# Other paces for the attention and layer-norm units woven into the wo and wb matmuls of an eight-core sandwich layer

## The chip, the cores and the metric

The kernel runs on the 8 cores of one Trainium2 chip. Each core handles 2048 of the 16384 tokens, with all the weights, and no core waits for another. The time is the device time of the slowest core in microseconds.

## The reference

```python
x = hidden_states                      # (4, 4096, 4096), fp32
h = layernorm(x)
q, k, v = h @ Wq.T, h @ Wk.T, h @ Wv.T # each (.., 64 heads, 64)
q, k, v = q * mask_q, k * mask_kv, v * mask_kv
scores = einsum('bshd,bsgd->bshg', q, k) / 8     # heads against heads, token by token
out = einsum('bshg,bsgd->bshd', softmax(scores), v)
x = x + layernorm(out @ Wo.T)
h = layernorm(x)
base = h @ W_base.T + b_base
# top-2 of 8 experts by h @ W_router.T, rank-16 LoRA per expert
lora = einsum('ter,te,eor->to', einsum('td,erd->ter', h, A), w, B) * 2
x = x + layernorm(base + lora)
```

The attention is between the 64 heads of one token, so each token stands alone. It is many small products: 64 x 64 scores per token.

## The kernel before

Each core works through its 2048 tokens in 2 chunks of 1024 (`for c in range(NCH)`), and each chunk in 8 tiles of 128 tokens (tau 0 to 7). LNT holds the chunk's normalised activations, transposed, in bf16. A weight matrix is read in 64 pieces: 8 column blocks of 512 (n) times 8 groups of 512 rows (ktg). A piece goes into one of four buffers WG. In chunk 0 a piece comes by a casting DMA from the fp32 weights on POOL and is saved as bf16 by SP (`s_wo<-WG`); in chunk 1, and in the second half of a chunk, it is read back by SP (`WG<-s_wo`). A group, below, is the set of matmuls with one piece: 32 matmuls of 128x512 in the QKV stage (L341), 16 in the wo stages (L590) and wb stages (L763), which take four tiles at a time and so four of the eight PSUM banks.

The stages of a chunk, in order:

- layer norm and transposes of all tiles, then the 192 QKV groups.
- attention of tiles 0 to 3 alone (`drain(a3_units(range(0, 4), 16, ...))`).
- first wo stage: 64 groups for tiles 0 to 3 (`proj_half`), and woven into it the attention of tiles 4 to 7 from the generator `gen_h1`, with what is left of it drained afterwards.
- second wo stage: 64 groups for tiles 4 to 7, and woven into it `a5_b0_units` for tiles 0 to 3 (two layer norms, transposes, router).
- first wb stage: six units of `moe_tail_units` (tile 4) ahead, then 64 groups for tiles 0 to 3; the rest of `moe_tail_units` (tiles 5 to 7 and the LoRA products) is woven into the first 8 groups, n = 0, and whatever is left is drained at the end of n = 0.
- second wb stage: 64 groups for tiles 4 to 7, with the final layer norm of tiles 0 to 3 (b6) beside them.

The weaving is by generators. Each `yield` ends a unit, and `drive(gen, k)` appends k units to the instruction lists after a group. There is no scheduler behind it: every engine runs its list in order and waits on semaphores, so the place of a unit in the lists decides which matmuls stand between two steps that depend on each other.

The attention of a tile has 54 units: two batches of 32 token pairs (bt = 0 and 1) of 26 units each, then the read of the result (`BFN<-on`, on POOL) and the transposes into LNT. A batch begins with one unit of eight DMAs on SP (QSG, KB and VB, L148) and ends with one unit that stores OB. Between them stand four waves of six units. The text calls the matmuls of a wave Q (L407), K (L427), S (L446), P (L487) and O (L506); the sixth unit has only VectorE's work on OB (L520). Q is copied to QBD by VectorE (L416), K to KTS by ScalarE (L435), S needs both; P waits for the maximum (L464) and the exponentials (L470); O waits for a copy by ScalarE (L494); the next Q waits for L520 of the wave before. Four tiles make 216 units.

A tile of `a5_b0_units` has six units: the reads of T2 and XT with the first layer norm; the residual sum, the store of xp and the second layer norm; the transposes (L278); the router logits (L645); the gating on VectorE (L651 to L672); the matmul and copy to WTS (L677, L680). The first read of T2 waits for every APST store of the wo stage before it.

After the eighth group of a column block ScalarE copies four banks to APST (L601), and POOL stores them; the units driven after that group come before these copies in the lists.

Of the kernel before, what the change touches and what calls it, by code (L numbers as in the profile page):

```python
# [26 lines left out]
def _build_program():  # L27
# [25 lines left out]
    ap_d = nc.dram_tensor("apn", [CH, DM], F32, kind="Internal").ap()  # L53
# [243 lines left out]
    for c in range(NCH):  # L297
      try:
# [257 lines left out]
        def drive(gen, k):  # L556
            for _ in range(k):
                if next(gen, "END") == "END":
                    return False
            return True  # L560

        def drain(gen):
            for _ in gen:
                pass
# [3 lines left out]
        a35h0_v, a35h0_s = cnt["V"], cnt["S"]  # L568
# [1 line left out]
        ph(4, c)  # L570
        ap_i = [0]

        def proj_half(nm, taus, banks, src, gen, img_d, first_waits=()):
            for n in range(NB):
                for ktg in range(8):
                    b, rdy = load_wgroup(nm, n, ktg, src)
# [16 lines left out]
                                 waits, inc="T" if (k4 == 3 and ti == len(taus) - 1) else None)  # L593
                    wg_done(b, "T", cnt["T"])
                    if gen is not None:
                        drive(gen, 3)
                tmm = cnt["T"]
                for ti, tau in enumerate(taus):
                    sl = ap_i[0] % 4
# [8 lines left out]

        gen_h1 = a3_units(range(4, 8), 8, (4, 5, 6, 7))
        proj_half("wo", [0, 1, 2, 3], [0, 1, 2, 3], src_kind0, gen_h1, ap_d,  # L610
                  [("V", a35h0_v), ("S", a35h0_s)])
        drain(gen_h1)
        g_set("LNTa", ("T", cnt["T"]))
        a4h0_ap = [(f"ap{i}", cnt[f"ap{i}"]) for i in range(4)]
        a4h0_vs = [("V", cnt["V"]), ("S", cnt["S"])]
# [69 lines left out]

        gen_a5h0 = a5_b0_units(range(0, 4), (0, 1, 2, 3))
        a4h1_ap = [None]
        proj_half("wo", [4, 5, 6, 7], [4, 5, 6, 7], "scratch", gen_a5h0, ap_d, a4h0_vs)
        a4h1_ap[0] = [(f"ap{i}", cnt[f"ap{i}"]) for i in range(4)]
        drain(gen_a5h0)  # L690
        g_set("LNTb", ("T", cnt["T"]))
# [51 lines left out]
        def b1_half(taus, banks, src, gen):  # L743
            for n in range(NB):
# [5 lines left out]
                for ktg in range(8):  # L750
# [16 lines left out]
                                 inc="T" if (k4 == 3 and ti == len(taus) - 1) else None)  # L767
                    wg_done(b, "T", cnt["T"])
                    if gen is not None:
                        drive(gen, 3)  # L770
                if gen is not None:
                    drain(gen)
                for ti, tau in enumerate(taus):
# [21 lines left out]
        gen_moe = moe_tail_units()  # L795
        drive(gen_moe, 6)
        b1_half([0, 1, 2, 3], [0, 1, 2, 3], src_kind0, gen_moe)
        drain(gen_moe)
        b1h0_y = [(f"ap{i}", cnt[f"ap{i}"]) for i in range(4)]
# [15 lines left out]

        b6_units(range(0, 4), b1h0_y)
        b1_half([4, 5, 6, 7], [4, 5, 6, 7], "scratch", None)
        g_set("LNTa", ("T", cnt["T"]))
        g_set("LNTb", ("T", cnt["T"]))
# [60 lines left out]
```

How the kernel before makes its waits and increments, by code:

```python
        def run(eng):  # L826
            for waits, fn, inc, amt in sched[name]:
                for s_, v_ in waits:
                    eng.wait_ge(sems[s_], v_)
                instr = fn(eng)
                if inc is not None:
                    instr.then_inc(sems[inc], amt)
```

## Time and profile before

| | us |
|---|---|
| median of 2 runs | 8694.74 |
| the runs | 8647.36, 8742.12 |
| profiled execution | 8209.84 |
| its span on the slowest core (core 7) | 8208.3 |
| spans of the eight cores | 8147.3 to 8208.3 |
| TensorE busy, share of the span | 5385.0, 66% |
| VectorE, ScalarE, POOL busy | 1492.6, 774.4, 496.2 |

The profile is one execution, taken apart instruction by instruction on the slowest core. The span runs from the first to the last instruction; the execution's own time is 1.5 us longer. The granted clock is the share of 2.4 GHz that TensorE was given: 1.00 is 2.4 GHz, 0.50 is 1.2 GHz, and a value between is a mean over time at both levels. An idle time in brackets stands before the first instruction of a row, with what ended it. The ends of matmuls are modelled, so that a matmul seems to overlap the next by a little.

### The profile page before, as it was taken

What the parts mean: (1) busy time and instruction counts of PE and PEld (TensorE: products, weight loads), DVE (VectorE), ACT (ScalarE), POOL (GpSimd) and SP (SyncE); (2) the same over time, 40 slices, a digit from 0 to 9 for tenths busy, and PEclk for the clock granted to TensorE, in tenths of its full rate; (3) what the DMA queues carried; (4) which work ended last, traced back from release to release, by engine and by line L of the source; (5) the groups of instructions that cost most, each with busy time, mean ns of one, the idle gap of its engine ahead of it and who ended that gap; (6) DMA issues with size and microseconds to landing.
All of it is one profiled execution on the core that took longest, in us unless ns stands there. A gap on an engine that the chain in (4) does not pass through costs nothing.

```text
span 8208.3 us, 69959 instructions; the slowest of 8 cores (8147.3 to 8208.3 us)
## 1 busy us (share of the span) xinstructions
PE 5385.0 (66%) x28056; PEld 2554.0 (31%) x28056; DVE 1492.6 (18%) x2144; ACT 774.4 (9%) x1427; POOL 496.2 (6%) x785
## 2 busy tenths in 40 slices
PE   4888888842345457564918888888822565476964
PEld 2333333322222223221403333333322232233321
DVE  4000000023212251302051000000033222504012
ACT  1000000012112210000010000000022122100000
POOL 1000000000001000111000000000000000000110
PEclk7999999965677778787958999999955787697987
DMA  6666666632566655797552222222222433555655
GB/s 149 141 146 144 141 144 141 141 76 52 96 137 133 133 192 185 174 197 233 173 205 71 77 77 77 77 77 77 77 49 52 113 102 94 196 183 163 213 184 191
DMA packets 940079, 1084.79 MB, mean 132 GB/s; under 512 B 575217, under 2 KB 792306, under 8 KB 923378
## 3 DMA queue, kind: packets, MB, share of 16 engines
q0 software_dynamic: 225872, 492.98, 26.3%
q1 hardware_dynamic: 713890, 587.34, 23.7%
q8 instruction: 229, 3.75, 0.2%
q14 instruction: 88, 0.72, 0.0%
HBM read 885.23 MB, written 369.10 MB: 153 GB/s over the span
## 4 chain that ended last, share of the span: by engine, by line
PE 58%; DMA 15%; DVE 11%; SPq 6%; ACT 6%; issue 3%; POOL 1%; DVEq 0%; ACTq 0%; POOLq 0%
PE PALL L341 33%; PE PALL L590 11%; PE PALL L763 8%; SPq L148 6%; DVE BN L192 4%; DMA WG<-wbT 2%; DMA T<-yn 2%; ACT QBD L494 2%; ACT PSTG L470 2%; DMA VB<-vn 2%; DMA T<-apn 1%; DMA WG<-woT 1%; PE PALL L278 1%; PE PALL L487 1%; PE PALL L407 1%
## 5 line engine op out<-in xcount | busy, mean ns | idle before, releaser
L341 PE MATMUL PALL<-WG,LNT 128*128 128x512 bf16 x12288 | 2787.8, 389 | 404.3 <-DVE QST L359 108.1
L341 PEld LDWEIGHTS PALL<-WG,LNT 128*128 128x128 bf16 x12288 | 1222.6, 100 | 1969.0 <-issue 601.5
L590 PE MATMUL PALL<-WG,LNT 128*128 128x512 bf16 x4096 | 1034.8, 413 | 190.0 <-DMA WG<-woT 92.2
L763 PE MATMUL PALL<-WG,LNT 128*128 128x512 bf16 x4096 | 937.7, 390 | 122.3 <-DMA WG<-wbT 113.6
L278 PE MATMUL PALL<-idt,BFN 128*128 128x128 bf16 x1536 | 168.9, 308 | 837.3 <-DVE BFN L204 608.8
L590 PEld LDWEIGHTS PALL<-WG,LNT 128*128 128x128 bf16 x4096 | 419.1, 105 | 747.9 <-issue 370.3
L763 PEld LDWEIGHTS PALL<-WG,LNT 128*128 128x128 bf16 x4096 | 404.5, 100 | 642.7 <-issue 203.3
L192 DVE BATCH_NORM_STATS2 BN<-T 128x6 f32<-128x512 f32 x320 | 193.5, 675 | 1695.4 <-DMA T<-yn 1244.9
L359 DVE TENSOR_TENSOR QST<-PALL,maskK 128x512 bf16<-128x512 f32 x128 | 80.7, 685 | 2053.6 <-PE PALL L341 2011.2
L278 PEld LDWEIGHTS PALL<-idt,BFN 128*128 128x128 bf16 x1536 | 158.6, 145 | 852.1 <-issue 852.1
L435 ACT ACTIVATE KTS<-PALL 128x512 bf16<-128x512 f32 x192 | 104.2, 594 | 3077.3 <-PE PALL L427 3077.3
L407 PE MATMUL PALL<-idt,QSG 128*128 128x128 bf16 x1024 | 103.7, 272 | 358.0 <-DMA VB<-vn 351.1
L416 DVE CAST QBD<-PALL 128x512 bf16<-128x512 f32 x256 | 162.0, 685 | 777.4 <-PE PALL L407 777.4
L487 PE MATMUL PALL<-idt,PSTG 128*128 128x128 bf16 x1024 | 102.6, 270 | 241.8 <-ACT PSTG L470 241.8
L359 DVE TENSOR_TENSOR QST<-PALL,maskV 128x512 bf16<-128x512 f32 x128 | 80.8, 685 | 987.9 <-PE PALL L341 950.3
L407 PEld LDWEIGHTS PALL<-idt,QSG 128*128 128x128 bf16 x1024 | 88.8, 125 | 378.6 <-issue 367.7
L470 ACT ACTIVATE PSTG<-PALL,NM 64x512 bf16<-64x512 f32 x256 | 167.8, 679 | 294.2 <-DVE NM L464 171.0
L481 DVE TENSOR_REDUCE ZW<-PSTG 128x8 f32<-128x1024 bf16 (+1 forms) x96 | 151.2, 1575 | 199.9 <-ACT PSTG L470 199.9
L290 DVE CAST LNT<-PALL 128x512 bf16<-128x512 f32 x192 | 132.9, 692 | 292.1 <-PE PALL L278 291.7
L785 ACT ACTIVATE APST<-PALL 128x512 f32<-128x512 f32 x128 | 76.2, 597 | 1037.6 <-PE PALL L780 1033.6
L148 POOL DMA_DIRECT2D BFN<-on x16 | 8.6, 536 | 2735.3 <-DMA on<-OB 2735.3
L776 PE MATMUL PALL<-bbn,onesb 1*128 1x512 bf16 x128 | 50.9, 398 | 181.6 <-DMA bbn<-bb 181.6
(99 smaller groups left out, 2149.3 us busy)
## 6 DMA issues: line engine op xcount, KB each, us to landing
WG<-s_wo SPq DMA_DIRECT2D x192, 512.0 KB, 3.6
WG<-s_wb SPq DMA_DIRECT2D x192, 512.0 KB, 3.8
XT<-x POOLq DMA_DIRECT2D x24, 2048.0 KB, 9.7
WG<-wqT POOLq DMA_DIRECT2D x64, 512.0 KB, 5.7
s_wq<-WG SPq DMA_DIRECT2D x64, 512.0 KB, 3.3
WG<-wkT POOLq DMA_DIRECT2D x64, 512.0 KB, 5.7
s_wk<-WG SPq DMA_DIRECT2D x64, 512.0 KB, 3.0
WG<-wvT POOLq DMA_DIRECT2D x64, 512.0 KB, 5.8
```

The lines of the kernel that those rows point to most:

```text
L148: return emit(eng, lambda e, o=out, i=in_: e.dma_start(out=o, in_=i), waits, inc=sem, amt=16)
L192: emit("vector", lambda e, i=i: e.bn_stats(BN[:, 6 * i:6 * i + 6], src_ap[:, 512 * i:512 * i + 512]), (list(vwaits) + g_w("MV") + g_w("BN" ...
L278: emit("tensor", lambda e, bk=bk, kt=kt, off=off: e.matmul(pb(bk, off * 128, 128), src_sb[:, kt * 128:kt * 128 + 128], idt[:], start=True, ...
L341: e.matmul(pb(tau, 0, 512), LNT[:, colk(kt, tau):colk(kt, tau) + 128], WG[b][:, k4 * 512:k4 * 512 + 512], start=st, stop=sp),
L359: ev = emit("vector", lambda e, tau=tau, sl=sl, mk=mk: e.tensor_tensor(QST[:, sl * 512:sl * 512 + 512].rearrange("p (h d) -> p h d", d=64) ...
L407: emit("tensor", lambda e, j=j, jj=jj, p=p, qb_bk=qb_bk: e.matmul(pb(qb_bk[j // 4], (j % 4) * 128, 128), QSG[p][:, jj * 128:jj * 128 + 128 ...
L416: emit("vector", lambda e, pw=pw, bk=bk, i_=i_: e.tensor_copy(QBD[pw][:, i_ * 512:i_ * 512 + 512], pb(bk, 0, 512)), [("T", t_s0)] if i_ == ...
L470: s_s6 = emit("scalar", lambda e, a=a, pw=pw, bk_i=bk_i, sb_=s_bk[bk_i]: e.activation(PSTG[pw][64 * a:64 * a + 64, bk_i * 1024:bk_i * 1024 ...
L487: emit("tensor", lambda e, j=j, pw=pw, ptb=pt_bk[j // 4], po=(j % 4) * 128: e.matmul(pb(ptb, po, 128), PSTG[pw][:, j * 128:j * 128 + 128], ...
L494: emit("scalar", lambda e, pw=pw, bk=bk, i_=i_: e.activation(QBD[pw][:, i_ * 512:i_ * 512 + 512], pb(bk, 0, 512), AF.Copy), [("T", t_s7)] ...
L590: e.matmul(pb(bk, 0, 512), LNT[:, colk(kt, tau):colk(kt, tau) + 128], WG[b][:, k4 * 512:k4 * 512 + 512], start=st, stop=sp),
L763: e.matmul(pb(bk, 0, 512), LNT[:, colk(kt, tau):colk(kt, tau) + 128], WG[b][:, k4 * 512:k4 * 512 + 512], start=st, stop=False), waits,
```

## The change

`proj_half` takes a number of units per group as an argument. The first wo stage drives 6 attention units after each group instead of 3, the second wo stage 1 layer-norm unit instead of 3, and the first wb stage 1 instead of 3. No instruction is added or removed; only the order of the lists changes.

```diff
-        def proj_half(nm, taus, banks, src, gen, img_d, first_waits=()):
+        def proj_half(nm, taus, banks, src, gen, img_d, first_waits=(), pace=3):
...
                     if gen is not None:
-                        drive(gen, 3)
+                        drive(gen, pace)
...
         proj_half("wo", [0, 1, 2, 3], [0, 1, 2, 3], src_kind0, gen_h1, ap_d,
-                  [("V", a35h0_v), ("S", a35h0_s)])
+                  [("V", a35h0_v), ("S", a35h0_s)], pace=6)
...
-        proj_half("wo", [4, 5, 6, 7], [4, 5, 6, 7], "scratch", gen_a5h0, ap_d, a4h0_vs)
+        proj_half("wo", [4, 5, 6, 7], [4, 5, 6, 7], "scratch", gen_a5h0, ap_d, a4h0_vs,
+                  pace=1)
...
                     if gen is not None:
-                        drive(gen, 3)
+                        drive(gen, 1)
```

TensorE, first wo stage of chunk 0, from the transposes of tile 3 on (one row of L590 x16 is one group; the names of the other rows are those given above), before:

```order
L278 MATMUL PALL<-idt,BFN 128x128 x32
L590 MATMUL PALL<-WG,LNT 128x512 x16
L407 MATMUL PALL<-idt,QSG 128x128 x8
L427 MATMUL PALL<-idt,KB 128x64 x8
L590 MATMUL PALL<-WG,LNT 128x512 x16
L446 MATMUL PALL<-KTS,QBD 128x64 x8
L487 MATMUL PALL<-idt,PSTG 128x128 x8
L506 MATMUL PALL<-VB,QBD 128x64 x8
L590 MATMUL PALL<-WG,LNT 128x512 x16
L407 MATMUL PALL<-idt,QSG 128x128 x8
```

The same place in the changed kernel:

```order
L278 MATMUL PALL<-idt,BFN 128x128 x32
L590 MATMUL PALL<-WG,LNT 128x512 x16
L407 MATMUL PALL<-idt,QSG 128x128 x8
L427 MATMUL PALL<-idt,KB 128x64 x8
L446 MATMUL PALL<-KTS,QBD 128x64 x8
L487 MATMUL PALL<-idt,PSTG 128x128 x8
L506 MATMUL PALL<-VB,QBD 128x64 x8
L590 MATMUL PALL<-WG,LNT 128x512 x16
L407 MATMUL PALL<-idt,QSG 128x128 x8
```

The group between K and S is gone; the one between O and the next Q stays.

TensorE, from the last transposes of the attention in the first wo stage of chunk 0 into the second wo stage, before:

```order
L506 MATMUL PALL<-VB,QBD 128x64 x8
L278 MATMUL PALL<-idt,BFN 128x128 x32
L590 MATMUL PALL<-WG,LNT 128x512 x16
L278 MATMUL PALL<-idt,BFN 128x128 x32
L590 MATMUL PALL<-WG,LNT 128x512 x16
L645 MATMUL PALL<-wrT_s,LNT 128x8 x32
L677 MATMUL PALL<-idt,WBF 8x128
L590 MATMUL PALL<-WG,LNT 128x512 x16
L278 MATMUL PALL<-idt,BFN 128x128 x32
```

and in the changed kernel:

```order
L506 MATMUL PALL<-VB,QBD 128x64 x8
L278 MATMUL PALL<-idt,BFN 128x128 x32
L590 MATMUL PALL<-WG,LNT 128x512 x496
L278 MATMUL PALL<-idt,BFN 128x128 x32
L590 MATMUL PALL<-WG,LNT 128x512 x16
L645 MATMUL PALL<-wrT_s,LNT 128x8 x32
L590 MATMUL PALL<-WG,LNT 128x512 x32
L677 MATMUL PALL<-idt,WBF 8x128
L590 MATMUL PALL<-WG,LNT 128x512 x48
L278 MATMUL PALL<-idt,BFN 128x128 x32
```

The 496 matmuls are 31 groups: 28 of the first wo stage, behind the end of the attention, and three of the second. In the second stage two groups now stand before L677 and three before the next tile's transposes, where one stood.

TensorE, first wb stage of chunk 0, from its first group to the LoRA products (L700 and L724, in the changed kernel L701 and L725), before:

```order
L763 MATMUL PALL<-WG,LNT 128x512 x16
L278 MATMUL PALL<-idt,BFN 128x128 x32
L763 MATMUL PALL<-WG,LNT 128x512 x16
L645 MATMUL PALL<-wrT_s,LNT 128x8 x32
L677 MATMUL PALL<-idt,WBF 8x128
...
L763 MATMUL PALL<-WG,LNT 128x512 x16
L700 MATMUL PALL<-WTS,rep 128x512 x2
L724 MATMUL PALL<-LNT,WG 128x512 x64
L763 MATMUL PALL<-WG,LNT 128x512 x16
```

and in the changed kernel:

```order
L764 MATMUL PALL<-WG,LNT 128x512 x48
L278 MATMUL PALL<-idt,BFN 128x128 x32
L764 MATMUL PALL<-WG,LNT 128x512 x16
L645 MATMUL PALL<-wrT_s,LNT 128x8 x32
L764 MATMUL PALL<-WG,LNT 128x512 x32
L677 MATMUL PALL<-idt,WBF 8x128
L764 MATMUL PALL<-WG,LNT 128x512 x32
L278 MATMUL PALL<-idt,BFN 128x128 x32
...
L677 MATMUL PALL<-idt,WBF 8x128
L701 MATMUL PALL<-WTS,rep 128x512 x2
L725 MATMUL PALL<-LNT,WG 128x512 x64
```

All eight groups of n = 0 now stand before the transposes of tile 6.

## Rows read from the trace of the kernel before

**Rows 1.** View of the cores: span and mean granted clock of the slowest.

```profile
core 7: 8208.3 us, clock 0.814
```

**Rows 2.** Windows of core 7: stretch, its length, busy time by engine, clock, DMA.

```profile
core 7: us, PE busy (x) PEld busy (x) DVE busy (x) ACT busy (x) POOL busy (x), PEclk, DMA share, GB/s
2139.00:2811.60 672.60, 344.25 (x2240) 172.04 (x2238) 122.98 (x180) 120.49 (x208) 61.72 (x91) 0.76 0.68 137
2811.60:2880.30 68.70, 17.36 (x193) 13.93 (x194) 19.15 (x28) 18.50 (x32) 3.78 (x7) 0.53 0.43 122
6384.60:6941.50 556.90, 341.35 (x2243) 168.46 (x2244) 122.99 (x180) 120.50 (x208) 16.58 (x31) 0.82 0.41 106
6941.50:7001.20 59.70, 16.80 (x193) 13.40 (x189) 19.15 (x28) 18.55 (x32) 3.73 (x7) 0.55 0.36 125
2880.30:3228.30 348.00, 253.03 (x1284) 118.78 (x1284) 100.00 (x160) 29.36 (x64) 20.25 (x38) 0.87 0.52 178
3275.00:3433.00 158.00, 68.41 (x398) 34.14 (x397) 78.05 (x125) 13.56 (x31) 17.66 (x26) 0.72 0.65 176
7395.70:7536.70 141.00, 69.77 (x398) 34.69 (x398) 77.80 (x125) 12.55 (x30) 6.30 (x10) 0.71 0.44 144
7173.40:7348.20 174.80, 168.53 (x766) 74.38 (x765) 0.00 (x0) 10.38 (x21) 11.91 (x23) 1.00 0.55 178
```

**Rows 3.** Timeline of TensorE, drained attention of chunk 1: start, length, instructions, idle before.

```profile
6961.68 1.01 PE L407 MATMUL PALL<-idt,QSG 128*128 128x128 bf16 x8 [1.22 <-DVE OB L520]
...
6964.35 0.58 PE L446 MATMUL PALL<-KTS,QBD 128*128 128x64 bf16 x8 [1.33 <-ACT KTS L435]
6967.35 1.01 PE L487 MATMUL PALL<-idt,PSTG 128*128 128x128 bf16 x8 [2.41 <-ACT PSTG L470]
...
6971.39 1.01 PE L407 MATMUL PALL<-idt,QSG 128*128 128x128 bf16 x8 [1.12 <-DVE OB L520]
```

**Rows 4.** Timeline of TensorE, first wo stage of chunk 1, batch with bt = 0.

```profile
6404.38 5.58 PE L590 MATMUL PALL<-WG,LNT 128*128 128x512 bf16 x16
...
6410.56 3.63 PE L590 MATMUL PALL<-WG,LNT 128*128 128x512 bf16 x16
...
6419.16 5.02 PE L590 MATMUL PALL<-WG,LNT 128*128 128x512 bf16 x16
```

**Rows 5.** Timeline of TensorE, same stage, batch with bt = 1.

```profile
6481.20 3.62 PE L590 MATMUL PALL<-WG,LNT 128*128 128x512 bf16 x16
...
6492.87 3.62 PE L590 MATMUL PALL<-WG,LNT 128*128 128x512 bf16 x16
```

**Rows 6.** Timeline, same stage, between the batches with bt = 0 and bt = 1.

```profile
6465.44 2.93 SPq L148 DMA_DIRECT2D VB<-vn  x2
...
6473.97 4.91 PE L590 MATMUL PALL<-WG,LNT 128*128 128x512 bf16 x16 [19.73 <-DMA WG<-s_wo]
```

**Rows 7.** Timeline, end of the last attention tile of chunk 1.

```profile
6980.92 1.70 SPq L148 DMA_DIRECT2D on<-OB  x2
...
6996.85 3.57 PE L278 MATMUL PALL<-idt,BFN 128*128 128x128 bf16 x32 [16.87 <-DMA BFN<-on]
```

**Rows 8.** Timeline of TensorE, chunk 0: first wo stage, then two column blocks of wb.

```profile
2420.43 5.86 PE L590 MATMUL PALL<-WG,LNT 128*128 128x512 bf16 x16 [14.47 <-DMA WG<-woT]
...
3532.12 9.83 PE L763 MATMUL PALL<-WG,LNT 128*128 128x512 bf16 x32 [11.72 <-DMA WG<-wbT]
...
3562.92 3.61 PE L763 MATMUL PALL<-WG,LNT 128*128 128x512 bf16 x16 [0.92 <-DMA WG<-wbT]
...
3581.05 9.27 PE L763 MATMUL PALL<-WG,LNT 128*128 128x512 bf16 x32 [11.96 <-DMA WG<-wbT]
```

**Rows 9.** Timeline, second wo stage of chunk 0 and what follows it.

```profile
2931.61 0.53 POOL L148 DMA_DIRECT2D T<-apn  x1
...
2939.66 3.57 PE L278 MATMUL PALL<-idt,BFN 128*128 128x128 bf16 x32 [17.71 <-DVE BFN L204]
...
2974.43 3.57 PE L278 MATMUL PALL<-idt,BFN 128*128 128x128 bf16 x32 [18.03 <-DVE BFN L204]
...
3265.87 3.57 PE L278 MATMUL PALL<-idt,BFN 128*128 128x128 bf16 x32 [37.52 <-DVE BFN L204]
```

## The prediction

> **What bounds the kernel now.** I read the view of the cores first: core 7 ends last, at 8208.3 us, with a mean granted clock of 0.814 [rows 1]; the profiled execution took 8209.84 us. All eight cores run the same program and lie within 61 us of each other, so one core can be read for all. Next I read the stages in windows [rows 2]. The change touches three stages of each chunk. In the wo stage of the first half (64 groups of 16 matmuls, with the attention of the other half woven in) the kernel spends 672.60 us and then 68.70 us in what is left of the attention (chunk 0), and 556.90 and 59.70 us (chunk 1). In the wo stage of the second half it spends 348.00 us, and in the first eight wb groups 158 us (chunk 0) and 141 us (chunk 1). The reader should set this against the dense stretch in rows 2: 174.80 us for 48 groups, 3.64 us a group, at a granted clock of 1.00. At that price 64 groups are 233 us, so the first wo stage is not a matmul stage. It is a chain: attention steps that wait for one another, with groups between them.
>
> How that chain is covered shows in the timeline. With no group in it a wave of eight heads takes 9.71 us from Q to Q, and TensorE waits 1.33 us for KTS and 2.41 us for the exponentials on its way [rows 3]. In the batches with bt = 0 the pace of 3 puts one group between O and the next Q, and one between K and S: 14.78 us a wave, in which the first group takes 5.58 us (it starts at the 1.2 GHz level after the light work) and the second 3.63 us (2.4 GHz level) [rows 4]. In the batches with bt = 1 the groups stand at S/P and at O/Q, and a wave with two groups takes only 11.67 us [rows 5]. So two groups there cost 2 us more than none: they are almost free.
>
> **The change: pace 6 in the first wo stage.** 216 units at 6 a group are gone after 36 groups instead of 64 groups and a drain of 24 units. So 28 groups lose their attention neighbours. I count what the attention part gets shorter by, and add the 28 groups.
>
> Batches with bt = 0, 16 waves in all four tiles: the group between K and S goes (3.6 us), but the wait for KTS and QBD that it hid comes back (1.4 us, after 1.33 in rows 3). 14.8 − 3.6 + 1.4 = 12.6 us, so 2.2 us less, 35 us in all.
>
> Batches with bt = 1: one group stays, between S and P. 9.71 − 2.41 (hidden) − 0.5 (P runs at the higher level) + 5.5 (a group that starts at the lower level, rows 4) = 12.3 us. Twelve waves stood at 11.67: +7 us. The four of the last tile ran without a group at 9.71: +10 us.
>
> Between bt = 0 and bt = 1 SP must first issue the store of OB and eight reads of 128-byte pieces. In chunk 1 the next group's weights are queued behind them on SP, so TensorE is idle 19.73 us and then runs that group before Q [rows 6]. After the change Q, K, S come first and need only the reads: the wait stays, the group (about 5 us) leaves it: −20 us over four tiles. In chunk 0 the weights come through POOL, the group lies in the shadow of the reads, and I count 0. At the end of a tile nothing changes: from the store of OB to the transposes pass 16 us of stores and reads [rows 7], in which TensorE has no part, so a group beside them neither shortens nor lengthens them.
>
> The 28 groups afterwards: in chunk 1 28 × 3.64 = 102 us. In chunk 0 each group needs a 1 MB cast load from POOL. The wb stage of chunk 0 shows what such groups cost with nothing woven in: from 3532.12 to the end of the eighth group, 3566.5, is 34.4 us, 4.3 each, and then TensorE waits 11.96 us at the column boundary, because the next loads stand on POOL behind four stores that wait for ScalarE [rows 8]. 28 × 4.3 = 120 us. The three boundaries among them are not new; before, the same boundary cost 14.47 us amid the attention [rows 8], so −6 us.
>
> Chunk 1: −35 + 7 + 10 − 20 + 102 = +64 us. Chunk 0: −35 + 7 + 10 − 6 + 120 = +96 us. Together +160 us.
>
> **Pace 1 in the second wo stage.** VectorE runs two layer norms a tile; from one tile's transposes to the next 34.77 us pass, and TensorE waits 18.03 us of them for BFN [rows 9]. Now one group stands between transposes and logits, two before WTS, three before the next transposes. The layer norms of the next tile are queued on VectorE behind the WTS copy, so the two new groups before WTS (7.5 us) delay them, less the 3.5 us of gating that they hide, plus 1 us for groups that start cold: 39.8 us a tile, but with 6 groups in it instead of 2. The first transposes come later: nothing is drained ahead, so T2 can only be read once the last APST stores have landed. The same chain from the end of the second wo stage takes 3265.87 − 3228.3 = 37.6 us [rows 9]. Fourth transposes at 37.6 + 3 × 39.8 = 157.0; then 3.6 for the transposes, 43 groups × 3.64 = 156.5 and 2.4 for logits, WTS and the cold start: 319.5 us against 348.0. −28.5 us a chunk, −57 us.
>
> A page of the Trainium skill speaks against me here: "SBUF — State Buffer", section "SBUF: two separate sides", says that a DMA issued from GpSimd cannot get its descriptors written while VectorE runs an operation of a two-port mode, and would put these loads behind the layer norms. In the trace the POOL DMAs beside the layer norms take 0.53 us, as everywhere [rows 9], and none waits for VectorE except where the program says so. By the page, up to 2.4 us would be lost at each of some eight cast loads of the wb stage in chunk 0, 20 us; by the row, nothing, and I take the row.
>
> **Pace 1 in the first eight wb groups.** The unit sequence must be drained at the end of n = 0 as before. Of the eight groups three now stand before the first transposes, one before the logits, two before WTS and two before the second transposes; the last two tiles run without any. Where VectorE's layer norms are waited for, groups cost nothing, before as after; what remains is that the last two groups of the eight (some 6 and 3.6 us by rows 4), which stood behind the last WTS and uncovered, are gone from there, against about 1 us more ahead of it: −9 us a chunk, −18 us. In chunk 0 POOL holds cast loads behind xp stores that wait for VectorE, before as after.
>
> **Sum.** 160 − 57 − 18 = +85 us on 8209.84. The median of the runs shown, 8694.74, is 1.059 of that execution; I scale the difference too: +90 us, 8785 us (+1.0%).
>
> **Rivals.**
> 1. *The groups stay at the higher level, not slower.* The one group a wave takes 5.5 us in my sum, and 3.6 us if the clock does not fall in the light work ahead of it. 72 groups × 1.9 = 137 us less: −52, scaled −55, 8640 us. It decides the sign: below 4.3 us a group the change does not lose. For it: the paced stretches of rows 5 keep 3.62 us. Against it: rows 4, where 5 us of light work were enough for a slow group, and rows 2, where the stretches of attention alone have 0.53 and 0.55.
> 2. *The groups run almost wholly at the lower level.* At 6.4 us each (twice 3.62 would be 7.2), 72 × 0.9 = +65: +150, scaled +159, 8854 us. For it: the light work between groups grows from 5 to over 7 us. Against: the group after the long wait in rows 6 takes 4.91. The Trainium skill's page "TensorE: Matmul & The Clock Gate", section "HAM oscillation — how this bites in real kernels", has this mechanism: bursts of sixteen matmuls parted by waits each start throttled again. By it every one of the 72 groups starts cold; my sum already has that, and the rival is only its full length.
> 3. *Pace 1 covers nothing in the second wo stage:* the layer norms slip by as much as the groups fill. Then 57 us are missing: +142, scaled +150, 8845 us. Against it stands the 18.03 us wait in rows 9, longer than three groups.
>
> **How the numbers follow.** Forecast 0.55, rival 1 0.17, rival 2 0.18, rival 3 0.10. The forecast's own range is 8725 to 8850: the 5.5 us may be 4.8 to 6.0, the reads of rows 6 vary by some us a batch, and the cast groups may cost 4.0 to 4.8 us. The whole range takes in rivals 1 and 2 with some room: 8630 to 8895. 2% of 8694.74 is 174 us, about what a measurement of this kernel tells from no change. Over it lie two thirds of rival 2 and a little of rival 3 and of the forecast: 0.17. Under −174 us only a case better than rival 1: 0.06. Within: 0.77.
>
> **What would show each step.** First wo stage of chunk 1 up to the end of its last group: 680 us by my sum (556.90 + 59.70 + 64), with the 28 dense groups at 3.64 us and 12 to 13 us from group to group before. Chunk 0: about 837 us in place of 741. Second wo stage: 320 us, with 40 us from transposes to transposes. Wb: the eighth group followed by n = 1 at 132 (chunk 1) and 149 us (chunk 0). I am wrong if the woven groups show 3.6 us, if the dense ones of chunk 0 run at the pace of chunk 1, or if the first wo stage gets shorter.

## The result and the profile after

The changed kernel takes 8501.22 us (median of 12 runs, 8297.42 to 8880.37), the kernel before, measured again beside it, 8531.78 us (median of 10 runs, 8217.97 to 8817.83). The ratio is 1.0096, with a 95% interval of 1.0077 to 1.0114: about 1% slower, which is no difference at the 2% bound; the two medians themselves differ by 31 us the other way. In many executions of either kernel the cores of one or both dies ran at a lower granted clock for a part of the time; the ratio leaves these out (among them the two runs shown before the prediction, 5% and 6% above the lowest), and where a stage below is given for some cores only, or a time is called the lowest, this is why.

In the profiled execution the cores of the changed kernel need 8252.6 to 8308.3 us, the ones of before 8147.3 to 8208.3 us. The view of the cores for the changed kernel (span and mean granted clock), against [rows 1]:

```profile
core 1: 8308.3 us, clock 0.806
...
die 0 (median of its cores): 8273.0 us, clock 0.809
die 1 (median of its cores): 8282.7 us, clock 0.808
```

The median over the eight cores is 8274.3 us against 8191.6 us: +83 us. The page of each kernel has the projections' matmuls in one group of its table of costly groups (instructions, busy us and mean ns of one, then idle time ahead of them). Before, then after:

```profile
L590 PE MATMUL PALL<-WG,LNT 128*128 128x512 bf16 x4096 | 1034.8, 413 | 190.0 <-DMA WG<-woT 92.2
```
```profile
L590 PE MATMUL PALL<-WG,LNT 128*128 128x512 bf16 x4096 | 1076.3, 426 | 161.1 <-DMA WG<-woT 103.1
```

The same 4096 matmuls are busy 41 us longer, and TensorE waits 29 us less ahead of them. This group mixes both wo stages, so it has to be taken apart by stage. Windows of core 1 of the changed kernel: chunk 0, first wo stage with attention woven in, then its dense tail; the same for chunk 1; the second wo stages of both chunks; the first eight wb groups with what is queued beside them, of both chunks. They answer to [rows 2].

```profile
core 1: us, PE busy (x) PEld busy (x) DVE busy (x) ACT busy (x) POOL busy (x), PEclk, DMA share, GB/s
2141.10:2813.00 671.90, 288.12 (x1984) 149.39 (x1984) 142.14 (x208) 130.74 (x224) 37.79 (x56) 0.67 0.48 94
2813.00:2978.20 165.20, 110.70 (x448) 45.35 (x448) 0.00 (x0) 8.26 (x16) 26.39 (x40) 0.83 0.93 199
6462.10:6993.80 531.70, 287.70 (x1984) 147.08 (x1985) 141.45 (x207) 129.96 (x223) 10.70 (x20) 0.71 0.34 84
6993.80:7098.70 104.90, 98.84 (x453) 43.50 (x451) 0.69 (x1) 9.04 (x18) 7.49 (x15) 1.00 0.52 169
2978.20:3306.00 327.80, 247.33 (x1284) 115.69 (x1284) 99.92 (x160) 29.00 (x64) 22.96 (x41) 0.88 0.58 202
7098.70:7422.50 323.80, 248.34 (x1284) 115.80 (x1284) 99.91 (x160) 29.00 (x64) 23.71 (x42) 0.88 0.61 207
3352.80:3518.20 165.40, 74.42 (x398) 33.91 (x398) 77.78 (x125) 13.45 (x31) 16.84 (x25) 0.65 0.64 166
7471.90:7607.90 136.00, 65.53 (x399) 33.62 (x398) 77.79 (x125) 13.31 (x31) 7.07 (x11) 0.70 0.47 145
```

The 448 matmuls of the second row are the 28 groups that lost their neighbours, the 453 of the fourth row the same in chunk 1. In chunk 1 they cost 104.90 us at a granted clock of 1.00 and a DMA share of 0.52. In chunk 0 they cost 165.20 us at 0.83, with the DMA engines 0.93 busy: not a matmul stage but a transfer stage.

The same stages for all runs, each number the median over the cores of the length of the stage in that trace (us; the stage bounds are read from the first and last copies of ScalarE and VectorE that end each stage; "attention" is the plain attention stage ahead of the wo stages; cores 0 to 3 for e3 and for the span of e8, 0 to 2 for e7; in e4 the first wo stage is that of cores 0, 1 and 4 to 7 in chunk 0 and of 2 to 5 in chunk 1; in e6 both wo stages of chunk 1 are those of cores 0, 1, 6 and 7):

| kernel | attention c0, c1 | first wo c0, c1 | second wo c0, c1 | 8 wb groups c0, c1 | span |
|---|---|---|---|---|---|
| before | 430, 408 | 736, 595 | 348, 348 | 142, 139 | 8192 |
| after | 429, 407 | 827, 634 | 331, 327 | 149, 133 | 8274 |
| e1 | 423, 413 | 818, 633 | 365, 363 | 142, 140 | 8319 |
| e2 | 423, 404 | 734, 589 | 311, 311 | 142, 141 | 8097 |
| e3 | 425, 413 | 736, 589 | 348, 347 | 150, 132 | 8169 |
| e4 | 423, 405 | 796, 629 | –, – | 141, 142 | – |
| e5 | 421, 406 | 808, 642 | 327, 324 | 148, 132 | 8238 |
| e6 | 331, 332 | 604, 548 | 348, 349 | 141, 142 | – |
| e7 | 421, 405 | 729, 583 | 359, 363 | 137, 144 | 8196 |
| e8 | 333, 331 | 602, 552 | 308, 308 | 143, 132 | 7748 |
| e9 | 422, 405 | 795, 631 | 331, 327 | 149, 132 | 8224 |
| e10 | 334, 333 | 573, 511 | 308, 307 | 143, 132 | 7684 |
| e11 | 288, 289 | 584, 509 | 310, 309 | 143, 132 | 7603 |

Between before and after the six touched stages give +90.5, +39.0, −16.8, −21.3, +7.8 and −6.8 us: +92 us, against +83 us in the span. All others stay within 10 us. The experiments ran on three chips: the kernel before took 8177.99, 8203.73 and 8204.52 us at the lowest beside e1 to e4, e5 to e8 and e9 to e11, and 8217.97 us beside the changed kernel. So whole times and spans of different rows can be compared to some 40 us only; the stages are the finer measure.

How the woven part looks now, from the timeline of core 1 of the changed kernel (start, length, instructions, idle time before): one wave with bt = 0, then the transition to bt = 1.

```profile
6500.03 6.36 PE L590 MATMUL PALL<-WG,LNT 128*128 128x512 bf16 x16
6506.22 0.61 PE L407 MATMUL PALL<-idt,QSG 128*128 128x128 bf16 x8
...
6508.48 0.39 PE L446 MATMUL PALL<-KTS,QBD 128*128 128x64 bf16 x8 [1.43 <-ACT KTS L435]
...
6511.29 0.61 PE L487 MATMUL PALL<-idt,PSTG 128*128 128x128 bf16 x8 [2.41 <-ACT PSTG L470]
...
6513.62 6.39 PE L590 MATMUL PALL<-WG,LNT 128*128 128x512 bf16 x16
...
6524.01 2.47 SPq L148 DMA_DIRECT2D VB<-vn  x2
...
6529.91 1.01 PE L407 MATMUL PALL<-idt,QSG 128*128 128x128 bf16 x8 [9.90 <-DMA VB<-vn]
6532.98 5.26 PE L590 MATMUL PALL<-WG,LNT 128*128 128x512 bf16 x16
```

From group to group are 13.59 us against 14.78 in [rows 4]; the group takes 6.36 us, where it took 5.58 and the second one 3.63. The wait for KTS is back (1.43 us). At the transition Q waits 9.90 us for the reads, no longer behind a group that itself waits 19.73 us for weights [rows 6].

### The profile page after: what moved, and what is told of

Same layout as the page of the kernel before. It is cut to its first block, busy times and chain, and to the rows that moved or that the text cites. A ratio compares the mean times of both kernels' runs of the same rounds, so it can differ in the third digit from the quotient of the medians.

```text
span 8308.3 us, 69958 instructions; the slowest of 8 cores (8252.6 to 8308.3 us)
## 1 busy us (share of the span) xinstructions
PE 5443.4 (66%) x28056; PEld 2566.3 (31%) x28056; DVE 1492.4 (18%) x2144; ACT 773.5 (9%) x1427; POOL 499.0 (6%) x785
## 3 DMA queue, kind: packets, MB, share of 16 engines
q8 instruction: 229, 3.75, 0.2%
## 4 chain that ended last, share of the span: by engine, by line
PE 57%; DMA 17%; DVE 11%; ACT 6%; SPq 5%; issue 4%; POOL 1%; DVEq 0%; ACTq 0%; POOLq 0%
PE PALL L341 33%; PE PALL L590 10%; PE PALL L764 8%; SPq L148 5%; DVE BN L192 4%; DMA WG<-wbT 3%; DMA T<-yn 3%; DMA WG<-woT 2%; DMA VB<-vn 2%; ACT QBD L494 2%; ACT PSTG L470 1%; PE PALL L278 1%; PE PALL L487 1%; PE PALL L407 1%; DMA T<-apn 1%
## 5 line engine op out<-in xcount | busy, mean ns | idle before, releaser
L590 PE MATMUL PALL<-WG,LNT 128*128 128x512 bf16 x4096 | 1076.3, 426 | 161.1 <-DMA WG<-woT 103.1
L590 PEld LDWEIGHTS PALL<-WG,LNT 128*128 128x128 bf16 x4096 | 432.4, 108 | 763.9 <-issue 409.9
L192 DVE BATCH_NORM_STATS2 BN<-T 128x6 f32<-128x512 f32 x320 | 193.5, 676 | 1930.2 <-DMA T<-yn 1284.9
```

The lines of the kernel that those rows point to most:

```text
L192: emit("vector", lambda e, i=i: e.bn_stats(BN[:, 6 * i:6 * i + 6], src_ap[:, 512 * i:512 * i + 512]), (list(vwaits) + g_w("MV") + g_w("BN" ...
L590: e.matmul(pb(bk, 0, 512), LNT[:, colk(kt, tau):colk(kt, tau) + 128], WG[b][:, k4 * 512:k4 * 512 + 512], start=st, stop=sp),
```

## The experiments

**e1: pace 6 alone.**

```diff
-        proj_half("wo", [4, 5, 6, 7], ..., a4h0_vs, pace=1)
+        proj_half("wo", [4, 5, 6, 7], ..., a4h0_vs, pace=3)
...
-                        drive(gen, 1)
+                        drive(gen, 3)
```

> Only the first wo stage at pace 6, the other two stages as before. Theory (the time comes from the first wo stage alone, the other two give a part back): that stage 92 us longer in chunk 0 and 40 us in chunk 1, as in the changed kernel, the others as before; +130 us in all, ratio 1.015 to 1.017. Rival (the paces act on one another, since a shorter drain makes the layer norms of the next stage start late): the second wo stage gets longer by 14 us a chunk because T2 can only be read after the last stores, ratio 1.018 to 1.020.

Measured: lowest time 8348.81 us, beside 8177.99 us of the kernel before on that chip (1.021). First wo stage +81.5 and +37.7 us, as in the changed kernel. The second wo stage, whose code is that of before, is 17.7 and 15.4 us longer: the rival was right. Core 3, windows of the second wo stage in both chunks:

```profile
2958.20:3323.70 365.50, 255.50 (x1284) 119.22 (x1284) 99.99 (x160) 31.47 (x69) 23.49 (x44) 0.84 0.53 183
...
7123.90:7484.50 360.60, 253.16 (x1284) 118.19 (x1284) 99.98 (x160) 31.40 (x68) 23.41 (x44) 0.85 0.52 186
```

So pace 6 has a second price, one stage on. With pace 3 the last units are drained behind the last group, and while they run, the layer norm's reads of the next stage can already land. With pace 6 nothing is left to drain: the stage starts with a layer norm whose input has just been stored, and its first transposes wait 34.84 us for BFN. Pace 6 in full: +152 us in the touched stages. The whole time says +171 us on that chip, and +128 us if the span is set against the trace of the kernel before, which was taken apart from these runs.

**e2: pace 1 in the second wo stage alone.**

```diff
-                  [("V", a35h0_v), ("S", a35h0_s)], pace=6)
+                  [("V", a35h0_v), ("S", a35h0_s)], pace=3)
...
-                        drive(gen, 1)
+                        drive(gen, 3)
```

> Only the second wo stage at pace 1. Here the attention is still drained ahead of it, so the first layer norm can begin earlier than in the changed kernel. Theory: the stage loses 18 to 23 us a chunk as in the changed kernel, and some 14 us more a chunk because its first transposes come at 23 to 27 us instead of 40 to 47; together -60 to -75 us, ratio 0.991 to 0.993. Rival (the gain is a matter of covering only, the late start costs nothing since groups fill it): -41 us, ratio 0.995.

Measured: lowest time 8126.89 us beside 8177.99 (0.994); the stage falls from 348 to 311 us in both chunks (−37 each, −74 together). Core 7:

```profile
2875.60:3188.60 313.00, 248.78 (x1284) 116.05 (x1284) 100.19 (x161) 29.71 (x66) 21.63 (x38) 0.90 0.56 200
...
6946.50:7257.40 310.90, 249.20 (x1284) 116.33 (x1284) 100.23 (x161) 29.70 (x66) 21.59 (x38) 0.90 0.58 206
```

The same 1284 matmuls, at a granted clock of 0.90 in place of 0.87 [rows 2]: groups stand in the 18 us for which TensorE waited for VectorE's layer norms [rows 9]. Rival 3 (pace 1 covers nothing) is out. Alone the edit is worth 37 us a chunk, beside pace 6 only 17 and 21.

**e3: pace 1 in the first eight wb groups alone** (paces 3 in both wo stages).

> Only the first wb stage at pace 1. Theory (chunk 0 loses because its cast loads stand on POOL behind the store of xp, chunk 1 gains because two groups no longer stand behind the last WTS): the first eight groups +7 us in chunk 0 and -7 us in chunk 1, ratio 0.999 to 1.001. Rival (my sum): -9 us in both, ratio 0.998.

Measured on cores 0 to 3: 150.2 us in place of 141.6 in chunk 0 (+8.6), 131.9 in place of 139.3 in chunk 1 (−7.4). The lowest time is 8194.43 us beside 8177.99. The edit is good where the weights come through SP and bad where they come through POOL. What happens there stands in the timeline of the changed kernel, chunk 0, core 1 (POOL's DMAs, TensorE's groups, VectorE's first layer norm instructions):

```profile
3367.78 0.54 POOL L148 DMA_DIRECT2D xp<-XT  x1 [22.46 <-DVE XT L626]
3368.31 3.00 POOL L148 DMA_DIRECT2D WG<-wbT  x4
...
3381.95 5.50 PE L764 MATMUL PALL<-WG,LNT 128*128 128x512 bf16 x16 [12.07 <-DMA WG<-wbT]
...
3407.96 4.85 DVE L192 BATCH_NORM_STATS2 BN<-T 128x6 f32<-128x512 f32 x8 [6.44 <-DMA T<-apn]
...
3417.54 6.47 PE L764 MATMUL PALL<-WG,LNT 128*128 128x512 bf16 x16 [12.84 <-DMA WG<-wbT]
```

POOL stands 22.46 us at a store of XT that waits for VectorE. Four loads of weights are issued directly behind it; the group that needs them waits 12.07 us, and the next tile's layer norm waits 6.44 us for a read of T that stands behind them. In the kernel before (core 7) POOL waits as long at this store, but only two loads are behind it, and the read of T follows at once:

```profile
3290.73 0.54 POOL L148 DMA_DIRECT2D xp<-XT  x1 [23.53 <-DVE XT L626]
3291.26 1.52 POOL L148 DMA_DIRECT2D WG<-wbT  x2
3292.74 0.59 POOL L148 DMA_DIRECT2D T<-apn  x1
```

**e4: is it the number of groups in a wave, or of places where they stand?** Here the first wo stage issues two groups together and then six units: as many places as with pace 6, but all 64 groups woven.

```diff
-                        drive(gen, pace)
+                        if ktg % 2 == 1: drive(gen, 6)
```

> The first wo stage only: two groups in a row, then six attention units, so that as many groups lie among the attention as before (the same 24 units are drained), but at one place of the wave instead of two. Other stages as before. Theory (what costs is that one place hides only one wait and that its first group starts at the lower clock level): a wave with a pair takes a one-group wave of the changed kernel (about 12.9 us) and 3.6 us more, 16.5 against a mean of 13.2 before; 28 waves, +80 to +95 us a chunk in the first wo stage, ratio 1.020 to 1.024. Rival (what costs is only that 28 groups were moved out of the attention to its end): the stage stays as before, ratio 1.000 to 1.004.

Measured: 796 us in chunk 0 and 629 us in chunk 1, so +60 and +34 us over before, where the changed kernel has +91 and +39, although here nothing is left over for a dense tail. Waves with a pair take 17.0 us with bt = 0 and 15.5 with bt = 1, against 15.6 and 11.6 us when the two groups stand apart (medians). It is less than the theory gave and far from nothing. So most of the loss of pace 6 is not one of fewer groups woven in: it is there with all 64, when a wave has one place for them instead of two. The whole times of e4 (8591.5 to 8866.07 us) allow no comparison, and its stages are read on the cores named at the table.

**e5: the eighth group's unit behind ScalarE's copies** (changed kernel; in the second wo stage the ninth group of each column block waited for the copies to APST, which stood on ScalarE behind a layer norm).

```diff
-                    if gen is not None:
+                    if gen is not None and ktg < 7:
                         drive(gen, pace)
...
                     g_set(f"APs{sl}", (f"ap{sl}", uv))
+                if gen is not None:
+                    drive(gen, pace)
```

> The changed kernel, but the units driven after the eighth group of a column block come behind ScalarE's four copies to APST instead of ahead of them. Theory (in the second wo stage the ninth group waited 13.5 us for a copy that stood on ScalarE behind the second layer norm, then ran uncovered): that stage 10 to 12 us shorter a chunk, 328 and 325 us become 317 and 314. In the first wo stage of chunk 0 the cast loads of the next block are no longer held up by six attention units: some 6 to 8 us at each of four boundaries, 25 to 30 us. In all -45 to -55 us against the changed kernel, ratio to before 1.003 to 1.006. Rival (the wait for the copies only stands in place of the wait for BFN): second wo stage unchanged, ratio 1.009 to 1.011.

Measured: second wo stage −3.9 and −2.9 us, where 10 to 12 were expected, and first wo stage of chunk 0 −19, where it was 25 to 30; lowest time 8260.33 us beside 8203.73 (1.007). The wait I had read was there in the changed kernel (core 1, second wo stage):

```profile
3019.80 3.57 PE L278 MATMUL PALL<-idt,BFN 128*128 128x128 bf16 x32 [31.04 <-DVE BFN L204]
...
3055.58 6.63 PE L590 MATMUL PALL<-WG,LNT 128*128 128x512 bf16 x16 [13.51 <-ACT APST L601]
```

It is gone in e5, but another stands in its place (core 1 of e5, VectorE):

```profile
7194.24 4.84 DVE L192 BATCH_NORM_STATS2 BN<-T 128x6 f32<-128x512 f32 x8 [5.47 <-DMA T<-apn]
```

The copies now come first, so their stores stand first on POOL, and the layer norm's read of T, issued behind them, comes late. A wait of 13.51 us was worth 3 us.

**e6: the kernel before, with the attention reads issued one batch ahead.** The change had made one thing visible: Q's wait for the reads of 128-byte pieces (9.90 us above, 19.73 in [rows 6]) is on the path at every batch, paced or not. The reads of the next batch are issued behind the first wave of this one; the two sets of buffers are those of before.

```diff
+        def rb_loads(tau, bt):
+            ...
+            rb_done[(tau, bt)] = cnt[f"rb{p}"]
...
+            if (tau, bt) not in rb_done:
+                rb_loads(tau, bt)
...
+                if w == 0 and (tau, bt) != (7, 1):
+                    rb_loads(*((tau, 1) if bt == 0 else (tau + 1, 0)))
                 yield
```

> The kernel before, at its own paces, with the eight reads of an attention batch issued one batch ahead, after the first wave of the batch before. Theory (the reads are a bare wait at the start of nearly every batch, 13 to 20 us each): attention stages 430 and 407 us become 330 and 310 (seven batches of about 15 us), first wo stages 736 and 595 become 640 and 510; -350 to -400 us, ratio 0.950 to 0.958. Rival (the descriptors of 128 bytes are the bound, and reads beside the weights take as much from them): half of that, ratio 0.975 to 0.985.

Measured: lowest 7854.44 us beside 8203.73, 0.957 of the kernel before. Attention −99 and −76 us, first wo stage −132 and −47 us. This is four times what the change under study costs.

**e7: the wb edit with its xp stores on SP** (pace 1 only in wb).

```diff
-                uq3 = dma("gpsimd", xp_d[row0...
+                uq3 = dma("sync", xp_d[row0...
```

> Only the first wb stage at pace 1, and every store of xp issued by SP instead of POOL. Theory (at pace 1 the cast loads of chunk 0 stand on POOL behind stores that wait for VectorE): the first eight groups of chunk 0 no longer lose 8.6 us but gain as in chunk 1, 150 us become 132 to 136; chunk 1 stays at 132; ratio 0.997 to 0.999. Rival (the order on POOL does not matter, the reads of T2 and the cast loads compete for the DMA engines): chunk 0 stays at 148 to 151, ratio 1.000.

Measured: the wb groups of chunk 0 take 136.9 us, against 150.2 in e3 and 141.6 before: the store's place on POOL is the cause of the loss in chunk 0, since taking it off removes the loss. Whether the weight loads or the read of T behind the store cost more, the run does not separate. But the stores now stand on SP ahead of weight reads: second wo stage 359 and 363 us (+12 and +15), wb groups of chunk 1 144.4 us. Lowest time 8220.49 us beside 8203.73, no gain. The store has to wait somewhere, and each queue has something behind it.

**e8: the edits that help, together.** e6, pace 1 in the second wo stage with the copies first, pace 3 in the first wo stage, and in wb pace 1 only in chunk 1.

```diff
-                        drive(gen, 1)
+                        drive(gen, 3 if c == 0 else 1)
```

> Reads ahead as in the sixth experiment, first wo stage at pace 3, second at pace 1 with the copies first, first wb stage at pace 3 in chunk 0 and 1 in chunk 1. Theory: the reads give 350 to 400 us, the second wo stages 37 us each as alone and some 8 us more each by the copies, wb 7 us; together -450 to -495 us, ratio 0.940 to 0.946. Rival (reads give half): 0.962 to 0.972.

Measured: lowest 7785.25 us beside 8203.73 (0.949), −418 us; somewhat less than expected. Second wo stage 308 us in both chunks (as e2 with 3 us more from the order of the copies), wb 143 and 132 us, first wo stage of chunk 1 552 us.

**e9: the APST stores of chunk 0's first wo stage on ScalarE's queue** (changed kernel). It asks whether the dense tail of 163 us is made by the cast loads behind the stores on POOL, or by the transfers.

```diff
-                    uv = dma("gpsimd", img_d[tau * 128:...
+                    uv = dma("scalar" if onact else "gpsimd", img_d[tau * 128:...
```

> The changed kernel, but in the first wo stage of chunk 0 ScalarE issues the stores of APST itself instead of POOL. Theory (at a column boundary the cast loads of the next block stand on POOL behind stores that wait for ScalarE's copies): the 28 groups behind the attention take 120 to 130 us instead of 163, the four boundaries inside the attention lose 5 to 10 us each; the stage 827 us becomes 750 to 775, other stages unchanged; ratio to the kernel before 0.999 to 1.002. Rival (the cast loads are bound by their own transfers, 1 MB read and half of it saved a group): the stage stays at 815 to 830, ratio 1.009 to 1.011.

Measured: 794.5 us in place of 826.7 (−32), of which some 22 in the part with the attention and 10 in the tail. Ratio to the kernel before 1.0065 (1.0036 to 1.0094). TensorE in the tail, the changed kernel (core 1), then e9 (core 4):

```profile
2840.89 16.73 PE L590 MATMUL PALL<-WG,LNT 128*128 128x512 bf16 x64 [12.86 <-DMA WG<-woT]
2861.71 16.56 PE L590 MATMUL PALL<-WG,LNT 128*128 128x512 bf16 x64 [4.09 <-DMA WG<-woT]
```
```profile
2847.55 0.38 PE L590 MATMUL PALL<-WG,LNT 128*128 128x512 bf16 x1 [1.37 <-DMA WG<-woT]
...
2864.60 16.00 PE L590 MATMUL PALL<-WG,LNT 128*128 128x512 bf16 x64 [5.57 <-DMA WG<-woT]
```

The wait for weights of 12.86 us at the column boundary falls to 1.37, but the one four groups later rises from 4.09 to 5.57 us. Over the tail the three boundaries lose 28 of their 37 us, and the tail only 9 (162 to 153 us, medians): the weights hardly come faster, with the DMA engines 0.93 busy before the edit and 1.00 after it (core 4, 2810 to 2965 us). Most of what the boundaries cost is transfer time that shows elsewhere when it does not show there; some 10 us are the order on POOL.

**e10: e8 with the groups put where the waits are.** With 26 units a batch, a pace of 3 puts the groups of bt = 1 at other places of the wave than those of bt = 0. Two yields a batch are taken out and one a tile put in, so that a wave has six units and a group always stands between S and P and between O and Q.

```diff
             rbq = (f"rb{p}", rb_done[(tau, bt)])
-            yield
...
-                yield
+                if w < nwav - 1:
+                    yield
...
                 g_set("BFN", ("T", cnt["T"]))
                 yield
+                yield
```

> The combined kernel of the eighth experiment, with the units regrouped so that at pace 3 both batches of a tile have their groups at S/P and at O/Q, as the batches with bt = 1 have: the empty first unit and the separate last unit of a batch go, one empty unit follows the transposes. Theory (where the groups stand, not how many, sets the price of a wave): waves of bt = 0 15.1 us become 12.2 to 12.9, first wo stages 602 and 552 us become 545 to 570 and 505 to 520; ratio to the kernel before 0.940 to 0.945. Rival (bt = 0 waves are longer for what stands around them): stages unchanged, ratio 0.949 to 0.952.

Measured: lowest 7720.39 us beside 8204.52 (0.941), 65 us below the lowest of e8, which ran on another chip; first wo stage 573 and 511 us (602 and 552), waves with bt = 0 in chunk 1 11.6 us (15.3, medians). One wave of e10 (core 3, chunk 1), one unbroken pattern of Q, S, group, P, O, group:

```profile
6088.08 0.61 PE L415 MATMUL PALL<-idt,QSG 128*128 128x128 bf16 x8
...
6090.35 0.39 PE L454 MATMUL PALL<-KTS,QBD 128*128 128x64 bf16 x8 [1.43 <-ACT KTS L443]
6090.57 3.62 PE L602 MATMUL PALL<-WG,LNT 128*128 128x512 bf16 x16
6094.03 0.61 PE L495 MATMUL PALL<-idt,PSTG 128*128 128x128 bf16 x8
6095.97 0.39 PE L514 MATMUL PALL<-VB,QBD 128*128 128x64 bf16 x8 [1.33 <-ACT QBD L502]
6096.19 3.62 PE L602 MATMUL PALL<-WG,LNT 128*128 128x512 bf16 x16
6099.65 0.55 PE L415 MATMUL PALL<-idt,QSG 128*128 128x128 bf16 x7
```

Q to Q are 11.57 us with two groups of 3.62 us. The same two groups cost 14.78 us a wave in [rows 4], where one of them takes 5.58 us. The number of groups is equal; only their places differ.

**e11: e10 with a tile's transposes behind the first wave of the next tile**, so that the store of OB and the read of BFN are hidden too [rows 7].

```diff
+                if w == 0 and pend_T:
+                    pend_T.pop()()
...
-                transpose_tile(BFN, ...)
+                pend_T.append(t_unit)
```

> The tenth experiment's kernel, and the transposes of an attention tile stand behind the first wave of the next tile, so that the store of OB and the read of BFN run beside a wave. Tile ends cost 24 to 33 us each before. Theory: 10 to 14 us less at each of 6 or 7 tile ends in all, and the 192 units fit the 64 groups exactly: attention stages 332 us become 290 to 300, first wo stages 500 to 530 in chunk 0 and 440 to 460 in chunk 1; ratio to the kernel before 0.915 to 0.925. Rival (in chunk 0 the read of BFN on POOL, which waits for the store, holds the cast loads longer in the new place): chunk 0 gains nothing in the wo stage, ratio 0.925 to 0.932.

Measured: lowest 7622.56 us, ratio 0.9308 (0.9256 to 0.9360): faster than both kernels, and in the range of the rival. Attention 288 and 289 us (from 333). But the first wo stages gain nothing: 584 us in chunk 0 (from 573), 509 in chunk 1 (from 511). Over four tiles the tile ends get 18 us shorter in chunk 1 and 23 in chunk 0, and the transitions from bt = 0 to bt = 1 get 8 and 37 us longer. Core 2, first wo stage with the attention ahead of it, both chunks:

```profile
1713.50:2589.40 875.90, 437.12 (x3840) 264.36 (x3840) 280.53 (x408) 237.81 (x415) 70.64 (x106) 0.74 0.72 140
...
5639.00:6438.60 799.60, 421.71 (x3840) 263.48 (x3840) 280.53 (x408) 238.16 (x416) 22.42 (x42) 0.76 0.47 112
```

In chunk 1 the DMA share is 0.47 over the stretch, in chunk 0 0.72. With the waits for reads gone the cast loads of chunk 0 are what is left, and reads and loads now meet in the DMA engines. That they slow one another there is inferred from these shares; no run separates them.

## Why the prediction was right and wrong

The forecast was +1.0%, the measurement is +0.96%; the sum was +85 us, the spans differ by +83 us. The time in us is wrong all the same: 8785 was forecast, with a range from 8630 to 8895, and 8501.22 was measured. One step did it: *"The median of the runs shown, 8694.74, is 1.059 of that execution; I scale the difference too"*. The two runs shown were both above 8640 us, the profiled execution at 8209.84. Measured again beside the changed kernel, before takes 8217.97 us in its lowest run, and the median over all its runs is 8531.78. I took two runs for the centre of a spread that reaches from 8218 to 8818 us, and my range let only the change vary, not the baseline. The gap of 6% between a profiled execution and the runs, with no other run between, was itself the warning. The range would have had to hold 8210 + 85 = 8295 us too.

Term by term, the sum came out by errors that cancel:

- **First wo stage, chunk 1, +64: measured +39.** Waves with bt = 0: −2.2 us a wave forecast, −2.4 measured (188.7 to 160.2 us over the twelve periods from wave to wave, 15.7 to 13.3 each). The group takes up to 6.4 us, not 5.5, but before, too, the mean wave was longer than the 14.78 of [rows 4]. Waves with bt = 1: +17 forecast, +4 measured; they take 11.9 us, not 12.3, and stood at 12.2 before, not 11.67. Transition: −20 forecast, −44 measured (139.1 to 94.6 over four), of which some 10 belong to the fourth wave of a batch. From the last read to Q now pass 3.4 us in place of 11.5 (medians). The group stood there, and ahead of it the wait for its own weights, which SP issues behind the reads; my sum took out the group and left the wait. Dense groups 102 forecast, 105 measured. The level I gave, 680 us, was on core 7, which had the longest such stage of all eight (617 us against a median of 595): one core does not stand for all in a single stage.
- **First wo stage, chunk 0, +96: measured +90, by errors that cancel.** Each of the seven column boundaries costs TensorE a wait of 10.3 to 12.3 us, before as after. Three of them moved out of the attention into the dense tail, so they are left out of the terms that follow; the sum had −6 for them, measured is 0. Waves with bt = 0: −2.2 a wave forecast, −1.7 measured (183.0 to 163.0 over twelve). Waves with bt = 1: +17 forecast, −5 measured. Transition: 0 forecast, −28 measured (131.9 to 104.1). *"The group lies in the shadow of the reads"* holds for the end, Q following the last read after 3.9 and 3.8 us. But the fourth wave is shorter, and SP issues the reads in 12.0 us in place of 14.4 (medians); I had neither. Tile ends: 0 forecast, +21 measured, mostly in the issue of the reads (22.0 us in place of 17.2 on average); why is open. Dense groups: 120 forecast, 125 measured, 4.5 us a group. With the three boundaries the tail takes 162 us, 5.8 a group, and e9 shows that this is mostly transfer time.
- **Second wo stage, −28.5 a chunk: measured −17 and −21.** The mechanism was right (e2: −37 alone). I had priced the late start, but took the periods as 39.8 us; they are 42, 37 and 45 us. The first has the copies to APST behind a layer norm on ScalarE in it and falls to 38 in e5; the other two stay, and what makes the third long was not tried. What pace 6 costs here was inside my sum as a first transpose at 37.6 us (measured 40); e1 shows it by itself, 15 to 18 us a chunk.
- **Wb, −9 a chunk: measured +8 and −7.** The step that failed: *"In chunk 0 POOL holds cast loads behind xp stores that wait for VectorE, before as after."* The order on the queue is the same, but not its place in time against the groups (e3, e7).
- **Rivals.** Rival 1 (groups at 3.6 us) and rival 2 (6.4 us throughout) are both out: over all woven groups the mean is 5.5 to 5.6 us, as the sum had it. Rival 3 is out by e2.

On the rule of "TensorE: Matmul & The Clock Gate" in the Trainium skill, section "HAM oscillation — how this bites in real kernels": the trace agrees, the groups of the timeline above, behind light work and waits, take 5.26 to 6.39 us against 3.62 in [rows 5], and e10 shows the way out, two groups a wave in the places S/P and O/Q, both at 3.62 us.

On "SBUF — State Buffer", section "SBUF: two separate sides", in the Trainium skill: I took the row against the page, and it was the wrong row. The DMA of [rows 9] is issued beside VectorE's L192; in the kernel before no issue on POOL falls into L204, the scaling at the end of a layer norm. In the changed kernel one store a chunk does, on every core, and the trace agrees with the page: its issue takes 1.87 us in place of 0.54 and ends 0.12 us after L204 (core 1; the first of these four):

```profile
3055.32 2.41 DVE L204 TENSOR_SCALAR BFN<-XT,NMR,RSTD 128x4096 bf16<-128x4096 f32 x1
3055.98 3.48 POOL L148 DMA_DIRECT2D apn<-APST  x4 [6.14 <-ACT APST L601]
```

It costs 1.3 us a chunk, so leaving it out of the sum did no harm; that no cast load fell into L204 was a matter of when the program issues them. What delayed the cast loads in chunk 0 was a wait that the program puts ahead of them, as e7 shows.

The three parts measured alone give 152 (e1), −74 (e2) and +1 (e3) us in the touched stages, together +79, against +92 in the changed kernel. The remaining 13 us are mostly chunk 0's first wo stage (827 against 818 in e1), whose cores lie 21 us apart; they stay open. The whole times of the three, +171, −51 and +16 us, add up to +136, which shows how coarse they are beside the stages.

## What to carry to other kernels

Where dense work is woven into a chain of short steps, ask in which waits of the chain it stands, not how much of it: in chunk 1 a wave took 11.6 us with two groups in the right places (e10), 13.3 with one between O and Q, and 17.0 with two together there (e4). Before moving a step ahead or behind, write down what stands behind it on each queue; waits on SP and POOL that moved with the pace are in most of the terms that missed here, and the largest gain (−99 and −76 us in the attention stages alone) came from issuing reads a batch ahead. And take the profiled execution and the runs apart before adding a difference to either: a level needs more than two runs.

## What the runs showed of the hardware that I had not expected

- What a group costs depends on where it stands. From e8 to e10 the instructions are the same and only the places move, and TensorE's busy time in chunk 1 falls from 464.08 to 433.33 us at a granted clock of 0.74 in place of 0.72 (attention and first wo stage, core 5 of e8, then core 3 of e10; on all cores 454 to 466 us, then 425 to 435). In the wave shown in e10 TensorE idles some 2.8 us and both groups still run at the 2.4 GHz level.

```profile
5714.30:6600.00 885.70, 464.08 (x3840) 277.97 (x3840) 281.78 (x408) 238.45 (x415) 22.43 (x42) 0.72 0.42 101
```
```profile
5686.20:6537.70 851.50, 433.33 (x3840) 265.31 (x3840) 281.56 (x408) 238.27 (x416) 22.42 (x42) 0.74 0.44 105
```

- 28 cast groups in a row, three column boundaries among them, take 5.8 us each with the DMA engines 0.93 busy at 199 GB/s; the same groups from the bf16 copies, in chunk 1, take 3.75 us each at a share of 0.52 and 169 GB/s. The share rises far more than the bytes.
- A wait removed on one queue mostly came back on another: 13.51 us on ScalarE were worth 3 us (e5), and stores moved from POOL to SP gave 13 us in one place and took 12 to 15 in two others (e7).
- What the issue of a DMA on POOL costs depends on VectorE's instruction at that moment. Into L204 it fell in e2, e5 and e8 to e11 as well, on every core, and took 0.97 to 1.87 us in place of 0.54, always ending 0.12 us after L204; a cast load in e7 took 2.45 us in place of 0.74. Beside VectorE's sum of XT and T (L626 in the kernel before), which is nearly twice as long, 48 stores each in e5, e8, e10 and e11 took 0.54 to 0.55 us.
